# Attention and mixture-of-experts block on one core: gates turned by VectorE in 32x32 blocks, the biases' product behind the first sums

## What is computed

```python
cont = flat @ W_s2c + b_s2c                                   # 2048 tokens x 64
probs = softmax(cont @ Wr + br)
topk_w, topk_idx = top_k(probs, 2)
topk_w = topk_w / sum(topk_w)
gate = sum(one_hot(topk_idx, E) * topk_w[..., None], axis=1)  # tokens x 8 experts, two not zero
h = relu(einsum('tm,emh->eth', cont, W1) + b1[:, None, :])
y = einsum('eth,ehm->etm', h, W2) + b2[:, None, :]
expert_out = einsum('etm,te->tm', y, gate)
spikes_moe = sigmoid(expert_out @ W_c2s + b_c2s)
decoded = spikes_moe @ W_dec + b_dec
return _layernorm(decoded, ln_g, ln_b)
```

## Time and profile before

| | us |
|---|---|
| median of 3 runs | 132.01 |
| lowest, highest | 131.33, 133.18 |
| the profiled execution | 131.94 |
| its span, first to last instruction | 130.1 |

### The profile page before, as it was taken

The page is one execution under the profiler, slowest core; times in us unless marked ns, Lnnn a source line. Parts: engine busy times, 40 slices in busy tenths (PEclk is TensorE's granted clock), DMA queues, the critical chain, the costliest instruction groups (busy, mean ns, idle before and its releaser), DMA issues.

```text
span 130.1 us, 2478 instructions
## 1 busy us (share of the span) xinstructions
PE 118.0 (91%) x813; PEld 79.4 (61%) x813; DVE 92.6 (71%) x392; ACT 61.3 (47%) x177; POOL 30.5 (23%) x61
## 2 busy tenths in 40 slices
PE   6899999999998999999999998999999999998400
PEld 2556686878645887663677983657566556665300
DVE  0858537698989755888246178968949996689792
ACT  1548764665838676104667660056641105705431
POOL 4423503325240213220000222233000043331531
PEclk9999999999999999999999999999999999999955
DMA  3558700000000019800000196000019759620202
GB/s 116 130 127 227 208 30 3 0 0 3 0 5 0 0 48 283 326 0 0 0 0 0 64 324 266 1 0 5 3 47 327 281 154 322 259 81 0 81 0 83
DMA packets 8843, 12.37 MB, mean 95 GB/s; under 512 B 2641, under 2 KB 5470, under 8 KB 8830
## 3 DMA queue, kind: packets, MB, share of 16 engines
q1 hardware_dynamic: 8190, 12.01, 28.5%
q10 hardware_dynamic: 640, 0.20, 0.7%
HBM read 11.09 MB, written 1.11 MB: 94 GB/s over the span
## 4 chain that ended last, share of the span: by engine, by line
PE 58%; DVE 19%; DMA 8%; POOL 4%; ACT 4%; issue 3%; POOLq 1%; SPq 1%; DVEq 0%
PE ps_t L905 9%; PE ps_s L760 7%; PE ps_o L785 6%; PE ps_s L881 5%; DMA gate_all<-gates 5%; PE ps_o L814 4%; POOL rstd L406 4%; PE ps_t L772 3%; DVE stats L1115 3%; PE ps_c L881 3%; PE ps_c L917 2%; PE ps_a L829 2%; DMA x_in<-in_L_attn_x 2%; DVE gated L1224 2%; ACT probs L495 2%
## 5 line engine op out<-in xcount | busy, mean ns | idle before, releaser
L406 POOL TENSOR_TENSOR rstd<-var_eps,minus_half 128x2 f32<-128x2 f32 (+1 forms) x33 | 25.4, 771 | 93.7 <-DVE var_eps L1120 45.8
L785 PEld LDWEIGHTS ps_o<-v,probsT 128*128 128x128 f32 x128 | 15.7, 191 | 3.5 <-ACT probsT L500 2.5
L785 PE MATMUL ps_o<-v,probsT 128*128 128x128 f32 x128 | 17.5, 279 | 0.1
L905 PE MATMUL ps_t<-gated,w 128*64 128x256 f32 x128 | 16.8, 389 | 0.6 <-DVE gated L1224 0.5
L495 ACT ACTIVATE probs<-ps_s,neg_max 128x512 f32<-128x512 f32 x16 | 11.0, 687 | 11.0 <-DVE neg_max L1143 10.4
L760 PE MATMUL ps_s<-xnT,yT 128*128 128x512 f32 x32 | 16.0, 596 | 0.1
L1143 DVE TENSOR_REDUCE neg_max<-ps_s 128x1 f32<-128x512 f32 x16 | 10.9, 689 | 6.0 <-PE ps_s L760 5.9
L905 PEld LDWEIGHTS ps_t<-gated,w 128*64 128x64 f32 x128 | 8.0, 136 | 8.4 <-DVE gated L1224 4.1
L1224 DVE SCALAR_TENSOR_TENSOR gated<-ps_s,b_minus,gate_all 128x512 f32<-128x512 f32 x14 | 9.9, 745 | 3.3 <-PE ps_s L881 1.8
L516 ACT ACTIVATE spikes<-ps_o,bias_half 128x512 f32<-128x512 f32 x6 | 4.1, 688 | 15.1 <-PE ps_o L814 15.1
L500 ACT ACTIVATE probsT<-ps_t 128x512 f32<-128x512 f32 x16 | 9.5, 592 | 2.0 <-PE ps_t L772 1.8
(11 more groups left out here) (184 smaller groups left out, 213.3 us busy)
## 6 DMA issues: line engine op xcount, KB each, us to landing
gate_all<-gates SPq DMA_DIRECT2D x12, 512.0 KB, 6.2
gate_all<-gates SPq DMA_DIRECT2D x8, 256.0 KB, 3.7
x_in<-in_L_attn_x SPq DMA_DIRECT2D x3, 256.0 KB, 3.8
w<-in_L_ffn_W SPq DMA_DIRECT2D x3, 256.0 KB, 4.2
out<-x_out SPq DMA_DIRECT2D x3, 256.0 KB, 2.0
x_in<-in_L_attn_x SPq DMA_DIRECT2D x2, 128.0 KB, 2.7
out<-x_out SPq DMA_DIRECT2D x2, 128.0 KB, 1.8
w_enc<-in_L_ffn_W_enc SPq DMA_DIRECT2D x1, 128.0 KB, 2.8
```

Source lines behind the costliest of these rows:

```text
L406: nc.gpsimd.tensor_tensor(rstd[part], var_eps[part], minus_half[:, t0:t1], ALU.pow).then_inc(g_rstd[n], 1)
L785: mm = nc.tensor.matmul(attn_out(t), probsT[:, b % 2, t, k], v[:, b % 2, k], start=(k == 0), stop=(k == T - 1))
L905: mm = nc.tensor.matmul(ps_t[h * M:(h + 1) * M, 0:SH], w2[:, e], gated[:, e, h * SH:(h + 1) * SH], start=False, stop=(e == E - 1))
```

## The change

The gates are no longer turned by PE. `gate` is now laid out with the experts ahead of the tiles, so that its 32 columns are contiguous, and DVE transposes it in blocks of 32x32 into `gate_blocks`: partition 32 j + (4 e + t) holds the gates of expert e for 32 tokens. ACT no longer copies anything; it issues the write straight from `gate_blocks`, 128 rows of 32 tokens (128 bytes each), to the same place in memory. `gateT`, which `expert_biases` needs, is fetched back by SP as a sixth transfer, between the second and the third of the others. In batches 2 and 3 SP's fetches wait in addition for the sums of two batches before (`pe_moe`), since they now overwrite `gateT`. `expert_biases` moves in batches 0 and 1 behind the fourth expert and in batch 2 behind the sixth; there it no longer starts the sum, the first `expert_out` does. In batch 3 it stays ahead of the first expert. `turn_gates` is gone in all four batches.

```diff
@@ SP
                 if b >= 2:
                     sp.wait_ge(v_gated, E * (b - 1))
+                    sp.wait_ge(pe_moe, b - 1)
+                else:
+                    sp.wait_ge(g_zero_rows, 4)
                 for j, (e0, e1) in enumerate(FETCHES):
+                    if j == 2:
+                        sp.dma_start(gateT[0:E, b % 2], gates_dram[b].ap()).then_inc(d_gateT[b % 2], 16)
                     sp.dma_start(gate_all[:, b % 2, e0:e1],
...
@@ ACT, gate_out
-                act.wait_ge(pe_gT, b + 1)
-                if b == 0:
-                    act.wait_ge(g_zero_rows, 4)
-                if b >= 2:
-                    act.wait_ge(d_gate_out[b - 2], 16)
-                nc.scalar.activation(gateT[0:E, b % 2], gates_bank(b)[0:E], ACT.Identity).then_inc(a_gT, 1)
-                act.wait_ge(a_gT, b + 1)
-                act.dma_start(gates_dram[b].ap(), gateT[0:E, b % 2]).then_inc(d_gate_out[b], 16)
+                act.wait_ge(v_gate_blocks, b + 1)
+                act.dma_start(gates_dram[b].ap().rearrange("e (t j r) -> j (e t) r", t=T, r=32),
+                              gate_blocks[:, b % 2]).then_inc(d_gate_out[b], 16)
@@ PE
-            def turn_gates(b):
...
+            def expert_biases(b):
+                pe.wait_ge(d_gateT[b % 2], 16 * (b // 2 + 1))
+                if b == 0:
+                    pe.wait_ge(v_b2, 1)
+                if b == B - 1:
+                    sum_bank(b)
                 for h in range(2):
                     nc.tensor.matmul(ps_t[h * M:(h + 1) * M, 0:SH], b2_plus[:, :], gateT[:, b % 2, h * SH:(h + 1) * SH],
-                                     start=True, stop=False)
+                                     start=(b == B - 1), stop=False)
...
@@ DVE, router_gates
-                nc.vector.tensor_tensor(gate[:, i], pick1[:, i], pick2[:, i], ALU.add).then_inc(v_gate, 2)
+                nc.vector.tensor_tensor(gate[:, i].rearrange("p e t -> p t e"), pick1[:, i], pick2[:, i],
+                                        ALU.add).then_inc(v_gate, 2)
+                dve.wait_ge(v_gate, count + 9)
+                if b >= 2:
+                    dve.wait_ge(d_gate_out[b - 2], 16)
+                nc.vector.transpose(gate_blocks[:, i], gate[:, i].rearrange("p e t -> p (e t)")).then_inc(v_gate_blocks, 1)
```

More of the change, by code:

```diff
@@ L127, in attention_moe_block @@
         pick2 = sb("pick2", [P, 2, T, E])
-        gate = sb("gate", [P, 2, T, E])
+        gate = sb("gate", [P, 2, E, T])
+        gate_blocks = sb("gate_blocks", [P, 2, E * T])
         gateT = sb("gateT", [P, 2, S])
@@ L207, in spikes2_bank @@
             return (ps_s if b == B - 1 and c else ps_c)[:, h, c * SH:(c + 1) * SH]
-        def gates_bank(b):
-            return ps_a if b == B - 1 else ps_c[:, 1]
         def token_halves(ap):
@@ L243, in attention_moe_block @@
         d_ln = sem("d_ln")
+        d_gateT = [sem(f"d_gateT{i}") for i in range(2)]
         d_gate_out = [sem(f"d_gate_out{b}") for b in range(B)]
@@ L275, in attention_moe_block @@
         pe_logit = sem("pe_logit")
-        pe_gT = sem("pe_gT")
         pe_h = sem("pe_h")
@@ L294, in attention_moe_block @@
         a_e2 = sem("a_e2")
-        a_gT = sem("a_gT")
         a_moe = sem("a_moe")
@@ L322, in attention_moe_block @@
         v_gate = sem("v_gate")
+        v_gate_blocks = sem("v_gate_blocks")
         v_gated = sem("v_gated")
@@ L859, in hidden_pair @@
                     if p == 1:
-                        pe.wait_ge(a_gT, b + 1)
+                        pe.wait_ge(v_logit, b + 1)
+                        pe.wait_ge(a_c2s, HC * b)
                     if p >= 2:
@@ L883, in hidden_pair, with sum_bank @@
                 mm.then_inc(pe_h, 1)
[L886 to L890, removed]
+            def sum_bank(b):
                 if b + 2 < B:
@@ L897, in expert_biases @@
                     pe.wait_ge(a_moe, b)
+            def expert_biases(b):
[4 more added lines that the diff above has]
+                    sum_bank(b)
                 for h in range(2):
                     nc.tensor.matmul(ps_t[h * M:(h + 1) * M, 0:SH], b2_plus[:, :], gateT[:, b % 2, h * SH:(h + 1) * SH],
-                                     start=True, stop=False)
+                                     start=(b == B - 1), stop=False)
             def expert_out(b, e):
+                first = e == 0 and b < B - 1
+                if first:
+                    sum_bank(b)
+                if b == 0 and e == 0:
+                    pe.wait_ge(d_w2, 32)
                 pe.wait_ge(v_gated, E * b + e + 1)
@@ L905, in expert_out @@
                     mm = nc.tensor.matmul(ps_t[h * M:(h + 1) * M, 0:SH], w2[:, e], gated[:, e, h * SH:(h + 1) * SH],
-                                          start=False, stop=(e == E - 1))
+                                          start=first, stop=(e == E - 1))
                 if e == E - 1:
@@ L1031, in _ @@
                     turn_h(n)
-                if more:
-                    turn_gates(b)
                 scores(m, 3)
-                if not more:
-                    turn_gates(b)
                 attend(m, 1)
@@ L1055, in _ @@
                 hidden_pair(b, 1)
-                expert_biases(b)
                 for e in range(4):
                     expert_out(b, e)
+                expert_biases(b)
                 hidden_pair(b, 2)
@@ L1075, in _ @@
             encode(3, 1)
-            turn_gates(2)
             decode(1, 0)
@@ L1084, in _ @@
             hidden_pair(2, 1)
-            expert_biases(2)
-            turn_gates(3)
             expert_out(2, 0)
@@ L1091, in _ @@
                 expert_out(2, e)
+            expert_biases(2)
             hidden_pair(3, 0)
```

## The result

| | before | after |
|---|---|---|
| median, us | 132.03 (22 runs) | 133.35 (22 runs) |
| lowest, highest | 131.13, 134.41 | 132.5, 136.92 |
| the profiled execution | 131.94 | 133.4 |
| its span | 130.1 | 131.5 |

The ratio after to before is 1.0095, with a 95% interval of 1.0070 to 1.0121: slower by about 1.3 us, within the 2% taken for no change. Some executions of most kernels here take over 1.5% longer than the fastest; the ratios leave them out and compare with runs of before made beside each kernel, while medians, lowest and highest are of all runs. The forecast was 133.0, in a range of 131.6 to 134.7.

What follows compares the result with a forecast made beforehand. PE was taken as the bound, busy 118.0 of 130.1 us. The running delay, +0.38 after batch 0 and +1.04 after batch 2, gave a span of 131.1, plus 1.84 around it: 133.0 us, range 131.6 to 134.7.

Steps and rivals of the forecast that it cites:

- The product: Biases' product behind the sums in batches 0 to 2: loses its cover and costs PE 0.48 us each time.
- Batch 0's turn: Removing PE's gate transposes in batch 0: saves 0.44 us, but DVE's delay leaves only −0.1.
- PE's turn of x follows it: Batch 0: PE's turn of x follows x_norm(3), which moves only from 46.09 to 45.98, so −0.1 is left.
- Batch 1: No gain from the turn, since attend(3, 1) waits for probsT; third landing 0.02 earlier; then the product, +0.48.
- The write's issue: Batch 1: ACT issues the gates' write behind probsT, at 70.92 instead of 71.37.
- rival 2: Gates' write takes 2.0 to 2.7 us, not 1.8, delaying batch 1's and 2's landings: 133.2 to 134.6 us; chance 0.15.
- Batch 2's turn: Removing PE's gate transposes in batch 2 saves 0.52 us, but DVE's delay brings route(3) at +0.26.
- Batch 2's landings: Experts 2 and 3 land at 101.8, DVE wants them at 102.0: hidden, by 0.2 us.
- the case named beforehand as wrong: The prediction is wrong if landings, not DVE, pace batch 2's sums; no size given.
- Batch 3: Product stays in front at 110.1; gateT's fetch hidden by about 1 us; no slack from there to the end.
- rival 4: gateT lands late in batch 3, so PE stands 1.4 us at the product: 134.4 us; chance 0.05.
- The sum: Whole span: 130.10 + 1.04 = 131.1 us, plus 1.84 around it: 133.0 us, 0.8% slower.

Runs made afterwards that it cites:

- the second profile: The changed kernel run again with no edit: median 132.99 us (6 runs), ratio to before 1.0124, profile span 130.4 us.
- e3: The kernel before with only the biases' product moved behind the sums in batches 0 to 2: median 133.11 us, ratio 1.0110.
- e9: The kernel before with batch 2's fetches cut to the first 256 of 512 tokens per expert: 131.73 us, ratio 0.9984.
- e10: The changed kernel with batch 2's fetches cut to the first 256 of 512 tokens per expert: 132.82 us, ratio 1.0079.
- the half-fetch pair: The kernels before and after, both with batch 2's fetches cut to 256 tokens per expert: after against before 1.0095.
- e4: The changed kernel writing a constant tile of 8 rows of 2 KB instead of the gates' 128 rows: median 132.87 us, ratio 1.0098.

## Why the prediction came out right, point by point

**The product** was priced at 0.48 each; from hidden pair to hidden pair it is 0.42 to 0.44. It is the cause shown by the runs: moved alone it costs 1.1%, moved back it returns 1.1 to 1.5%.

**Batch 0's turn** was mis-sized: −0.36 beside the −0.1 forecast (−0.45 in the ledger, of which −0.09 was there at scores(2, 0), 37.39 and 37.30). The step that failed is "PE's turn of x follows it". DVE's part was near: `x_norm(3)` came at 45.83 and was taken to come at 45.98. But what follows on PE does not hang on it alone. ACT's xnT stands behind the squares of the attention in its queue and starts without idle time at 47.42 in after, 47.86 in before: the attention came 0.44 earlier, and with it xnT. The path was through ACT, not through DVE and POOL.

**Batch 1.** attend(3, 1) at ACT's probsT, as forecast, so the turn gave nothing. The write's issue was wrongly placed behind probsT (70.92): ACT's queue issued at 70.23, 0.25 behind the start of the transpose, while probsT ran from 69.90. The write was under-sized, 1.95 and not 1.8 (batch 0: 2.01, batch 2: 2.24). By its size that is the lower end of rival 2, but at the place where it would have cost, the earlier issue had made room for it. The two errors are of opposite sign: in batch 1 0.69 earlier and 0.15 longer. From SP's first fetch to the third tile on DVE it was 7.30 (72.18 to 79.48) against 6.89 (72.83 to 79.72), 0.41 more where 0.09 was set for gateT; in the second profile it was 7.06 (71.94 to 79.00), and with the old five fetches in e3 6.35 at most (73.53 to 79.88, no wait). With 0.54 between two profiles of the old fetches, gateT's price stays open. The net was 0.24 earlier where 0.02 was forecast, and that too lies within this scatter. Then came the product.

**Batch 2's turn** gave 0.51 (forecast 0.52), and route(3) came at +0.14 where +0.26 was forecast: DVE's step from the gates' sum to z_centre went from 0.11 (92.81 to 92.92) to 0.50 (93.01 to 93.51), 0.39 more where 0.30 was set, on a start that was earlier by the errors above. In batch 3's routing the transpose lengthened the step from the gates' sum to the first gated tile from 0.13 to 0.38 (100.02 to 100.40), 0.25 more. 0.30 lies between the two. The write of batch 2 was not issued "as before" but 0.86 earlier (93.50 and 94.36): the prediction took off only ACT's copy, but the wait for PE's turn is gone with it, so that from the gates' sum to the issue it is 0.49 and not 1.55. The write then took 2.24 and not 1.8, and the first fetch went out 0.08 earlier than before. Here too one error covered the other.

**Batch 2's landings** were forecast hidden by 0.2, and only the third fetch (experts 2 and 3) was worked out. The one that came late was the fourth (experts 4 and 5), 0.77 in one profile and not at all in the other. The margin of the third was overstated as well: two gated tiles take 1.33 from start to start (99.91 to 101.24 with half fetches), not the 1.41 of their row, so in before, with 100.01 and 101.47, DVE already stood 0.13 for it, and with 1.33 the working gives a margin of 0.07. That landings pace batch 2's sums is the case named beforehand as wrong, and it does occur, as scatter. By e9 and e10 it is not what makes the median. A margin of 0.2 was too thin to be called hidden.

**Batch 3.** No wait of PE for gateT at the product (110.36), as forecast; rival 4 did not happen. From there to the end both kernels run alike: 1.36 later at the product, 1.4 at the end.

**The sum.** +1.04 was forecast. The profile has +1.4 with the chance landing, the medians 1.3 and the half-fetch pair 0.9 to 1.1. Part of the agreement is luck: batch 0's turn gave 0.26 more than forecast, the products 0.13 less, batch 1's third landing helped by 0.22 more than forecast, which e3 shows to be within scatter, and what batch 2's landing took stands against them. The kernel with the product in front says what the rest of the change is worth: the turns gained back on PE, less the transpose and the slower write, come to −0.2% and −0.1%, with intervals from −0.6 to +0.2%: nothing that can be told from no change. A version of it that beats before for certain was not found.

## What to carry to other kernels

Ask of a short independent product what it covers: ahead of a run of sums that another engine paces it is free, behind them it costs its whole length each time. Work taken off the busiest engine pays only where that engine would not wait next anyway; here four turns were removed, and with the product left in front the time stayed within 0.6% of before. Before speeding up what leads to a stage that uses fetched data, look at how close the landings are: a lead of DVE of half a microsecond came back as waits for transfers. And read no gain from a wait that is gone in one profile: batch 1's was gone in a kernel that fetches exactly as before, too.

## What the runs showed of the hardware that was not expected

- A write of 16 KB took, from its issue to the issue of the fetch that waits for it, 1.94 to 2.02 us in batches 0 and 1 and 2.16 to 2.44 in batch 2 as 128 rows of 128 bytes, and 1.46 to 1.48 as 8 rows of 2 KB, but 2.04 in batch 2 of the changed kernel with eight rows (e4, 92.99 to 95.03). Cutting it in four over two queues did not shorten it beyond 0.16 (1.85, 1.97 and 2.85).
- The last of the 16 increments of a fetch of 512 KB came 0.1 us behind the fifteenth in one profile (e3, batch 1's third fetch) and 1.1 behind it in another (before, the same fetch). What waits for the fetch waits for the last.
- Issued while fetches of megabytes are queued, a small write waits with them: batch 3's took 4.27 (100.51 to 104.78), before 2.70 (101.39 to 104.09), as eight rows in the changed kernel 4.51 (99.99 to 104.50), with half fetches 1.46 (e9) and 1.93 (e10).
- ACT's queue issues a transfer while an activation that stands ahead of it still runs (70.23, within probsT from 69.90 for 0.60; in batch 0 at 44.12, ahead of the starts of the two activations before it in ACT's order, 44.16 and 44.63).
- DVE's transpose of 128x32 in float32 takes 0.21, and adds 0.25 to 0.39 on the path of what follows. The gates' sum ahead of it, whose output is now written with a stride, takes 0.21 or 0.22 (69.73, 100.02), not 0.19.
